# A two-pass mixture-of-experts block on one core: half tiles of two experts share a slot, in two column tiles of TensorE

## The chip, the cores and the metric

One core of a Trainium2 chip. The time of a run is the device time of the whole program in microseconds (us); all arithmetic on the path described here is float32.

## The reference, cut to what matters

The input is `x`, 4096 tokens (2 sequences of 2048) of 256 channels. Three layers follow one another, each on a layer-normed input and added to it:

```python
x = x + 0.5 * ffn(layernorm(x))     # mixture of 8 experts, one per token
x = x + recurrence(layernorm(x))    # 256 -> 64, three gated linear recurrences along the sequence, 64 -> 256
x = x + 0.5 * ffn(layernorm(x))     # the same mixture again

def ffn(x):                         # tokens xt [4096, 256]
    probs = softmax(xt @ Wr + br);  gate = max(probs);  idx = argmax(probs)
    h = relu((layernorm(xt) * ln_g + ln_b) @ W1[idx] + b1[idx])  # 256 -> 1024
    return (h @ W2[idx] + b2[idx]) * gate                        # 1024 -> 256
```

The inputs fix which expert each token gets. Worked out from the reference, tokens of each expert after each quarter of both sequences (the kernel's classes 0 to 3):

```text
first ffn     expert 0   1     2    3     4    5   6    7
  after c=0          95    8   366    7   503    0   0   45
  after c=1         173   12   768   10   993    1   0   91
  after c=2         252   13  1169   13  1483    2   0  140
  after c=3         332   17  1583   15  1969    2   0  178
second ffn
  after c=0          76   12   430    5   449    0   0   52
  after c=1         138   19   834    7   949    0   0  101
  after c=2         201   22  1229    9  1463    1   0  147
  after c=3         265   27  1637    9  1972    1   0  185
```

## The kernel before, in words

**Routing.** For every class of 1024 tokens (512 of each sequence) the kernel computes router logits on TensorE (`transposes`, `logits`, `turn_logits`), the argmax and the token's rank among its expert's tokens (`choose` L808, `ranks` L1583, `place` L846 on VectorE), and scatters the token rows into a region per expert in DRAM (`routed_rows`): `route` L641, four parts of two indirect DMAs each, issued by POOL. `counts` and `keep_counts` give the running counts per expert.

**Slots.** An FFN pass works in slots of 128 rows of one expert. `tables` (L871, six parts on VectorE) writes for each slot its expert, its first row and a mask for rows that are not there. Slots come in stages, so that a pass can begin before all classes are routed: `EARLY` gives the slots of the early stages, (9) in pass 0 and (4, 9, 8) in pass 1; the last stage takes what is left, partly filled tiles among it. Each stage's tables need the routing of one more class (in pass 0: classes 0 and 1, then all).

In slot `i`, SyncE loads the rows (`slot_rows` L460, ring of 5) and 1 MB of first weights (`slot_weights` L467, ring of 3 buffers, so the load of slot i waits for the first product of slot i-3); the second weights of all 8 experts stay in SBUF. VectorE normalises (`norm` L1171); TensorE transposes the 128x256 tile (`turn_input` L1686, L1692); ScalarE applies gain and offset (`affine`, L1431). TensorE's first product (L1705) holds a 128x128 block of weights and moves the 128 rows, so the hidden layer comes out with its channels on partitions; ScalarE and VectorE add the bias and clip, half each (`activate`, L1441 and L1185), and the second product (L1719) holds a block of the hidden layer and moves 256 columns of the second weights. VectorE adds the bias, the gate and the residual (`finish` L1189), and POOL scatters the rows to `x_middle` or the output (`store`, L655). TensorE's order in a slot is: transposes of slot i+1, first product of i, second product of i-1. Every float32 matmul is two records in the trace, a transpose is one.

**Order of the rest.** Everything else is "beside work": routing, tables and the recurrence (down projection `down` L1595, gates L1603, `project`, `norms`, `spread`, `up`, with `convolve`, `gate_input`, `scan` on VectorE). Lists of numbers at the top (L22 to L69) place each step by hand: a slot has a place (`PLACE`), a place is 2 steps on VectorE, ScalarE and POOL (before and behind the activation, on POOL behind the first half of the first product) and 8 on TensorE (behind each quarter of the two products), and each step is divided in `SUB` = 24. So 1704 on POOL is step 71, the second half of place 35. At a stage boundary TensorE holds back half of the last second product until the next stage's first rows are there (`begin_stage` L1737); SyncE waits for the stage's tables before its first weights (`next_weights` L476) and for its scatters before its first rows (`next_rows` L481), in order with all else in its queue. The recurrence begins at place 20 of pass 0 and ends in pass 1's early stages; its results of class c must be routed before pass 1's stage c begins. The banks 4 to 7 and the buffer `rec` belong to the beside work.

## Time and profile before

| | |
|---|---|
| runs before | 711.96, 714.51, 716.04 us, median 714.51 |
| profiled execution | 711.34 us, span of the trace 709.6 us |
| TensorE busy | 658.8 us, 93% of the span |
| VectorE, ScalarE, POOL busy | 409.5, 271.4, 172.2 us |
| mean granted TensorE clock | 0.966 |
| first products (L1705) | 2368 records, 286.9 us busy |
| second products (L1719) | 1184 records, 276.3 us busy |
| weights, 1 MB each | 82 loads by SyncE, median 5.2 us from issue to landing |

TensorE's busy time is that of its matmul records, which overlap; the chain of waits shows how far apart they really start. The span is from the first to the last instruction; the device time has 1.7 us more.

### The profile page before, as it was taken

What the parts mean: (1) busy time and instruction counts of PE and PEld (TensorE: products, weight loads), DVE (VectorE), ACT (ScalarE), POOL (GpSimd) and SP (SyncE); (2) the same over time, 40 slices, a digit from 0 to 9 for tenths busy, and PEclk for the clock granted to TensorE, in tenths of its full rate; (3) what the DMA queues carried; (4) which work ended last, traced back from release to release, by engine and by line L of the source; (5) the groups of instructions that cost most, each with busy time, mean ns of one, the idle gap of its engine ahead of it and who ended that gap; (6) DMA issues with size and microseconds to landing.
All of it is one profiled execution on the core that took longest, in us unless ns stands there. A gap on an engine that the chain in (4) does not pass through costs nothing.

```text
span 709.6 us, 15541 instructions
## 1 busy us (share of the span) xinstructions
PE 658.8 (93%) x4420; PEld 576.8 (81%) x4420; DVE 409.5 (58%) x1427; ACT 271.4 (38%) x642; POOL 172.2 (24%) x177
## 2 busy tenths in 40 slices
PE   7649999999999999999998979999799999999993
PEld 5548888999978878797777857889589989999992
DVE  7756672333355677777787757787567623333331
ACT  4214221332235656544654437554343223222220
POOL 4733443111111121033302330124212521111111
PEclk9559999999999999999999999999999999999998
DMA  8969785865563544437336164423553666452530
GB/s 287 303 200 394 275 269 184 264 204 164 189 222 129 169 150 142 142 88 242 101 99 232 70 237 144 150 82 120 178 202 133 196 200 203 152 202 96 178 125 14
DMA packets 59920, 126.51 MB, mean 178 GB/s; under 512 B 8106, under 2 KB 36661, under 8 KB 59701
## 3 DMA queue, kind: packets, MB, share of 16 engines
q1 hardware_dynamic: 53204, 108.50, 46.7%
q0 software_dynamic: 6624, 16.92, 6.5%
q8 instruction: 42, 0.69, 0.4%
q14 instruction: 50, 0.40, 0.2%
HBM read 106.36 MB, written 20.35 MB: 179 GB/s over the span
## 4 chain that ended last, share of the span: by engine, by line
PE 66%; DVE 12%; issue 7%; DVEq 5%; DMA 3%; POOL 2%; ACT 1%; SPq 0%; POOLq 0%; ACTq 0%
PE bank L1705 30%; PE bank L1719 28%; PE bank L1692 2%; POOL routed_rows L646 2%; DMA pay<-routed_rows 2%; DVE st L759 2%; DVEq L400 1%; DVE rec L1095 1%; PE bank L1642 1%; PE bank L1609 1%; DVE act_t L1185 1%; DVE rec L1071 1%; PE bank L1616 1%; DVE y_b L1194 1%; PE bank L1547 1%
## 5 line engine op out<-in xcount | busy, mean ns | idle before, releaser
L1705 PE MATMUL bank<-mn_t,w 128*128 128x128 f32 x2368 | 286.9, 277 | 3.9 <-ACT mn_t L1431 1.9
L1705 PEld LDWEIGHTS bank<-mn_t,w 128*128 128x128 f32 x2368 | 276.2, 193 | 15.3 <-issue 10.3
L1719 PE MATMUL bank<-w,act_t 128*128 x1184 | 276.3, 383 | 5.7 <-DVE y_b L1194 5.3
L1719 PEld LDWEIGHTS bank<-w,act_t 128*128 128x128 f32 x1184 | 218.2, 191 | 42.8 <-issue 17.0
L1431 ACT ACTIVATE mn_t<-bank,vec 128x128 f32<-128x128 f32 x152 | 61.5, 455 | 242.6 <-PE bank L1692 242.6
L1185 DVE TENSOR_SCALAR act_t<-bank,vec 128x128 f32<-128x128 f32 x296 | 83.3, 344 | 104.0 <-PE bank L1705 89.8
L1441 ACT ACTIVATE act_t<-bank,vec 128x128 f32<-128x128 f32 x296 | 84.9, 369 | 69.4 <-PE bank L1705 69.3
L1194 DVE TENSOR_TENSOR y_b<-bank,b_all 128x256 f32<-128x256 f32 x74 | 31.4, 425 | 105.4 <-PE bank L1719 94.7
L655 POOL DMA_INDIRECT x_middle<-res,pay x37 | 36.9, 997 | 216.9 <-DVE res L1201 182.2
L655 POOL DMA_INDIRECT out_x<-res,pay x37 | 36.9, 996 | 205.8 <-DVE res L1201 171.8
L646 POOL DMA_INDIRECT routed_rows<-rows,dest x64 | 64.6, 1010 | 56.3 <-PE bank L1705 27.1
L1176 DVE TENSOR_SCALAR mn<-pay 128x256 f32<-128x256 f32 x78 | 31.8, 408 | 20.7 <-DMA pay<-routed_rows 20.3
L1692 PE MATMUL bank<-ident,mn 128*128 128x128 f32 x152 | 30.3, 282 | 13.9 <-DVE mn L1176 9.2
L638 POOL TENSOR_TENSOR inv_std<-var_eps,minus_half 128x16 f32<-128x16 f32 (+1 forms) x12 | 31.0, 2581 | 48.6 <-DVE var_eps L769 35.0
L1201 DVE SCALAR_TENSOR_TENSOR res<-y_b,pay 128x256 f32<-128x256 f32 x74 | 35.8, 484 | 7.2
L1692 PEld LDWEIGHTS bank<-ident,mn 128*128 128x128 f32 x152 | 20.4, 145 | 22.7 <-issue 9.7
L759 DVE BATCH_NORM_STATS2 st<-rows 128x6 f32<-128x256 f32 x96 | 33.7, 414 | 2.6 <-DMA rows<-in_L_attn_h 0.7
L1071 DVE SCALAR_TENSOR_TENSOR rec<-seq,lay,rec 128x512 f32<-128x512 f32 x36 | 27.0, 749 | 2.0 <-issue 0.2
L1335 ACT ACTIVATE xn_t<-bank 128x512 f32<-128x512 f32 x32 | 17.9, 604 | 18.8 <-PE bank L1547 18.7
L1547 PE MATMUL bank<-ident,rows 128*128 128x128 f32 x128 | 20.4, 312 | 0.7 <-ACT xn_t L1335 0.6
L1547 PEld LDWEIGHTS bank<-ident,rows 128*128 128x128 f32 x128 | 17.2, 163 | 3.5 <-issue 2.4
L1373 ACT ACTIVATE rec<-bank,lay 64x512 f32<-64x512 f32 x24 | 16.4, 683 | 9.5 <-PE bank L1609 9.2
(212 smaller groups left out, 459.7 us busy)
## 6 DMA issues: line engine op xcount, KB each, us to landing
w<-in_L_ffn_W SPq DMA_DIRECT2D x82, 1024.0 KB, 5.2
pay<-routed_rows SPq DMA_DIRECT2D x78, 130.0 KB, 2.1
rows<-in_L_attn_h SPq DMA_DIRECT2D x8, 512.0 KB, 7.0
rows<-x_middle SPq DMA_DIRECT2D x8, 512.0 KB, 5.1
routed_rows<-fill SPq DMA_DIRECT2D x2, 1040.0 KB, 7.7
routed_rows<-rows,dest POOLq DMA_INDIRECT x64, 3.5
b_all<-in_L_ffn_b SPq DMA_DIRECT2D x1, 1024.0 KB, 12.0
x_middle<-res,pay POOLq DMA_INDIRECT x37, 2.6
```

The source lines that it names most:

```text
L646: g.indirect_dma_start(out=routed[f], out_offset=bass.IndirectOffsetOnAxis(ap=dest[:, t:t + 1], axis=0), in_=rows[:, t * RW:(t + 1) * RW], ...
L655: g.indirect_dma_start(out=x_out if p else x_mid, out_offset=bass.IndirectOffsetOnAxis(ap=pay[p][i % RING][:, C_ID:C_ID + 1].bitcast(I32), ...
L759: v.bn_stats(st[:, jj * 6:jj * 6 + 6], tile_of(c, b, j, 0, D))
L1185: last = v.tensor_scalar(act_t[i % 2][:, c * P:(c + 1) * P], b_hid[1][:, c % 4 * P:(c % 4 + 1) * P], vec[:, ds(eb + c, 1)], 0.0, ALU.add, ...
L1194: v.tensor_tensor(y_b[i % 2][:, :], b_out[i % 2], b2_all[:, ds(eb * (D // FC), D)], ALU.add).then_inc(m_yk[p], 1)
L1201: v.scalar_tensor_tensor(out=res[p][i % 2][:, :], in0=y_b[i % 2][:, :], scalar=a[:, C_GATE:C_GATE + 1], in1=a[:, 0:D], op0=ALU.mult, op1=A ...
L1431: last = a.activation(mn_t[p][i % 2][:, k * P:(k + 1) * P], b_in[i % 2][:, k * P:(k + 1) * P], ACT.Identity, scale=vec[:, V_G + k:V_G + k ...
L1441: last = a.activation(act_t[i % 2][:, c * P:(c + 1) * P], b_hid[0][:, c * P:(c + 1) * P], ACT.Relu, bias=vec[:, ds(eb + c, 1)])
L1547: last = t.transpose(bk[cc][n % 2][:, j * P:(j + 1) * P], tile_of(c, b, j, k * P, P), ident[:, :])
L1692: last = t.transpose(b_in[i % 2][:, k * P:(k + 1) * P], mn[p][i % 2][:, k * P:(k + 1) * P], ident[:, :])
L1705: last = t.matmul(b_hid[half][:, c % 4 * P:(c % 4 + 1) * P], w1[i % W1S][:, k * F + c * P:k * F + (c + 1) * P], mn_t[p][i % 2][:, k * P:(k ...
L1719: last = t.matmul(b_out[i % 2], act_t[i % 2][:, c * P:(c + 1) * P], w2[:, ds(eb * (WE // FC) + c * D, D)], start=c == 0, stop=c == FC - 1)
```

## The change

Per pass, three slots become pair slots (`PAIR_AT`: the second, fifth and eighth slot of the last stage). A pair slot takes 64 rows of each of two experts. A new function `pairs` in front of the last tables finds the experts whose remaining number of 64-row halves is odd, orders them ahead of the others, and gives the first six of the order one half each; the rest of the tables is made from what is left. The early stages are (7) and (5, 9, 8) instead of (9) and (4, 9, 8).

In a pair slot the first product turns round: the rows are stationary (64 columns for each expert) and the weights move, 512 columns at a time, each expert in its own column tile (output partitions 0 to 63 and 64 to 127). The hidden layer comes out with its rows on partitions, is copied raw to `rec` (`keep_hidden`), turned by 8 transposes into banks 4 and 5 (`turn_hidden`), and then gets bias and relu in 64-column pieces, since the two halves have different biases (`activate_pair`, in the next slot). The second product has 64 stationary columns per expert, again in two column tiles; the second expert's second weights are loaded once more into `rec` (1 MB), the first's are in place. A pair slot loads two first-weight buffers of the ring. All lists of places are written anew with `SUB` = 96.

```diff
-SUB = 24
+SUB = 96
...
-R_SCATTER = [[[None, None, None, None], [None, None, None, None], [72, 120, 168, 216], [264, 312, 360, 408]],
-    [[1560, 1608, 1656, 1704], [2040, 2088, 2136, 2160], [2472, 2520, 2568, 2616], [2856, 2904, 2952, 3000]]]
-TABLE_PARTS = [[[None, None, None, None, None, None], [169, 192, 240, 264, 288, None]], [[1584, 1609, 1633, 1682,
-    1683, 1728], [2066, 2088, 2112, 2113, 2116, 2281], [2497, 2544, 2568, 2569, 2593, 2616], [2881, 2904, 2905,
-    2952, 2953, None]]]
+R_SCATTER = [[[None, None, None, None], [None, None, None, None], [289, 480, 481, 672], [673, 864, 865, 1056]],
+    [[6240, 6432, 6433, 6624], [8544, 8545, 8640, 8641], [10272, 10464, 10465, 10560], [11232, 11424, 11425,
+    11616]]]
+TABLE_PARTS = [[[None, None, None, None, None, None], [577, 768, 864, 960, 1056, None]], [[6433, 6528, 6624, 6626,
+    6720, 6722], [8546, 8640, 8641, 8642, 8644, 8645], [10369, 10464, 10560, 10562, 10563, 10564], [11329, 11520,
+    11616, 11712, 11808, None]]]
...
-    EARLY = ((FULL,), (4, 9, 8))
+    HALF = P // 2
+    PAIRS = 3
+    HALVES = 2 * PAIRS
+    PAIRED = HALVES * HALF
+
+    EARLY = ((FULL - 2,), (5, 9, 8))
...
+    PAIR_AT = [[FIRST[p][-1] + 1 + 3 * k for k in range(PAIRS)] for p in range(FFNS)]
...
+        w2_b = rec[:, 0:WE]
+        raw_h = rec[:, WE:WE + F]
+        b_turn = [bank[4], bank[5]]
...
+            def pair_second_weights(p, i):
+
+                k = PAIR_AT[p].index(i)
+                eb = expert_of_half(sp, p, i, 1)
+                if k:
+                    sp.wait_ge(m_y[p], PAIR_AT[p][k - 1] + 1)
+                sp.dma_start(w2_b.rearrange("p (c d) -> p c d", c=FC),
+                             w2_rows[ds(eb * (F // FC), F), :].rearrange("(c p) d -> p c d", p=P)).then_inc(s_w, 16)
...
+            def pairs(f):
...
+                v.tensor_scalar(odd_i, odd_i, HALF.bit_length() - 1, 1, ALU.logical_shift_right, ALU.bitwise_and)
...
+                v.scalar_tensor_tensor(out=key, in0=odd, scalar=float(2 * E), in1=e_desc[:, :], op0=ALU.mult, op1=ALU.add)
...
+                    if last:
+                        pairs(f)
...
+            def keep_hidden(p, i):
+                dve.wait_ge(m_h[p], halves_before(p, i) + 2)
+                v.tensor_copy(raw_h[:, F // 2:F], b_hid[1][:, :]).then_inc(m_a[p], 1)
+
+            def activate_pair(p, i):
+                experts = [expert_of_half(dve, p, i, h) for h in range(2)]
+                dve.wait_ge(m_h[p], halves_before(p, i) + 4)
+                for c in range(FC // 2, FC):
+                    for h in range(2):
+                        lo = h * HALF
+                        last = v.tensor_scalar(act_t[i % 2][:, c * P + lo:c * P + lo + HALF],
+                                               b_turn[1][:, c % 4 * P + lo:c % 4 * P + lo + HALF],
+                                               vec[:, ds(experts[h] + c, 1)], 0.0, ALU.add, ALU.max)
+                last.then_inc(m_a[p], 1)
...
+                if is_pair(p, i):
+                    k = q % 2
+                    for h in range(2):
+                        on = slice(h * HALF, (h + 1) * HALF)
+                        lo = k * P + h * HALF
+                        last = t.matmul(b_hid[half][on, :], mn_t[p][i % 2][:, lo:lo + HALF],
+                                        w1[loads[h] % W1S][:, k * F + half * (F // 2):k * F + (half + 1) * (F // 2)],
+                                        start=k == 0, stop=k == KD - 1)
...
+            def turn_hidden(p, i):
+
+                for half in range(2):
+                    pe.wait_ge(m_a[p] if half else m_b[p], activations_before(p, i) + 1)
+                    for c in range(FC // 2):
+                        o = half * (F // 2) + c * P
+                        last = t.transpose(b_turn[half][:, c * P:(c + 1) * P], raw_h[:, o:o + P], ident[:, :])
+                    last.then_inc(m_h[p], 1)
...
+                    for c in range(q * 2, q * 2 + 2):
+                        t.matmul(b_out[i % 2][0:HALF, :], act_t[i % 2][:, c * P:c * P + HALF],
+                                 w2[:, ds(eb * (WE // FC) + c * D, D)], start=c == 0, stop=c == FC - 1)
+                        last = t.matmul(b_out[i % 2][HALF:P, :], act_t[i % 2][:, c * P + HALF:(c + 1) * P],
+                                        w2_b[:, c * D:(c + 1) * D], start=c == 0, stop=c == FC - 1)
```

`keep_hidden` and `activate_pair` have twins on ScalarE for the first half of the hidden layer. `turn_hidden` stands on TensorE behind the second product of the slot before. Divided by `SUB`, the scatters of class 1 in pass 1 stood in steps 85, 87, 89 and 90 and now stand in 89, 89, 90 and 90, with the boundary's step being 90 in both; those of class 2 stood in 103, 105, 107 and 109 and now in 107, 109, 109 and 110, the boundary's step being 110. The tables of the same classes ended their part 4 in steps 88 and 108, and now do so in 90 and 110. In pass 0 the scatters end in step 11 instead of 17, and the tables' part 0 stands in step 6, before slot 3's activation, instead of step 7, behind it.

## Rows read from the trace of the kernel before

**Rows 1.** Stretches: us, busy PE, PEld, DVE, ACT, POOL; PE clock; DMA
```profile
197.00:381.00 184.00, 178.82 (x1200) 147.92 (x1198) 132.34 (x412) 99.07 (x199) 38.50 (x32) 1.00 0.46 153
381.00:424.00 43.00, 38.95 (x254) 32.90 (x255) 28.79 (x107) 18.42 (x42) 13.19 (x13) 0.95 0.46 160
...
513.50:694.30 180.80, 179.70 (x1239) 166.03 (x1237) 78.36 (x275) 52.27 (x153) 33.55 (x32) 1.00 0.51 166
```

**Rows 2.** Chain of waits, a quiet stretch; start us, us, what
```profile
614.79 3.57 PE bank L1705 x32
618.36 3.46 PE bank L1719 x16
621.82 0.22 PE bank L1692 x2
622.04 3.57 PE bank L1705 x32
```

**Rows 3.** The page's groups of instructions
```profile
L1441 ACT ACTIVATE act_t<-bank,vec 128x128 f32<-128x128 f32 x296 | 84.9, 369 | 69.4 <-PE bank L1705 69.3
...
L655 POOL DMA_INDIRECT x_middle<-res,pay x37 | 36.9, 997 | 216.9 <-DVE res L1201 182.2
L655 POOL DMA_INDIRECT out_x<-res,pay x37 | 36.9, 996 | 205.8 <-DVE res L1201 171.8
...
L1335 ACT ACTIVATE xn_t<-bank 128x512 f32<-128x512 f32 x32 | 17.9, 604 | 18.8 <-PE bank L1547 18.7
```

**Rows 4.** Chain of waits around the first down projection
```profile
202.04 0.87 PE bank L1547 x8
202.91 1.79 PE bank L1705 x16
204.70 1.87 PE bank L1599 x8
...
207.56 1.09 PE bank L1705 x8
```

**Rows 5.** Instructions of the down projection (L1599)
```profile
L1599 PEld LDWEIGHTS bank<-xn_t,down_t x32: 133/136/137, 204.6 to 407.8; 128*64 128x64 f32 x32
L1599 PE MATMUL bank<-xn_t,down_t x32: 592/592/643, 204.6 to 408.3; 128*64 128x512 f32 x32
```

**Rows 6.** Chain of waits, an up projection in two row tiles
```profile
290.81 1.06 PE bank L1642 x8
```

**Rows 7.** Timeline of VectorE, 44 to 125 us
```profile
55.44 0.23 DVE L838 TENSOR_TENSOR hit<-hit,e_desc 128x64 f32<-128x64 f32 x1
55.73 0.22 DVE L840 TENSOR_REDUCE first<-hit 128x8 f32<-128x64 f32 x1
...
77.07 0.41 DVE L1176 TENSOR_SCALAR mn<-pay 128x256 f32<-128x256 f32 x1 [1.86 <-DMA pay<-routed_rows]
...
81.24 0.19 DVE L906 TENSOR_TENSOR seg_x<-cnt,done 128x32 f32<-128x32 f32 x1
...
102.65 0.24 DVE L969 TENSOR_SCALAR tab_off<-slot_v,part_no 128x30 int32<-128x30 f32 x1
```

**Rows 8.** Timeline of TensorE, 80 to 130 us
```profile
81.28 3.74 PE L1705 MATMUL bank<-mn_t,w 128*128 128x128 f32 x32
```

**Rows 9.** Timeline of SyncE's queue, 40 to 125 us
```profile
118.78 2.92 SPq L465 DMA_DIRECT2D pay<-routed_rows  x3
```

**Rows 10.** Timeline of POOL, 404 to 426 us
```profile
411.79 0.98 POOL L646 DMA_INDIRECT routed_rows<-rows,dest  x1 [0.31 <-issue]
```

**Rows 11.** Timeline of SyncE's queue, 404 to 426 us
```profile
413.52 1.52 SPq L472 DMA_DIRECT2D w<-in_L_ffn_W  x2
415.88 2.54 SPq L465 DMA_DIRECT2D pay<-routed_rows  x3
```

**Rows 12.** Timeline of VectorE, 404 to 426 us
```profile
422.68 0.41 DVE L1176 TENSOR_SCALAR mn<-pay 128x256 f32<-128x256 f32 x1 [4.21 <-DMA pay<-routed_rows]
```

**Rows 13.** Waits of TensorE; us in total, times, longest
```profile
PE bank L1692 <- issue: 4.7, 2, 2.4
```

More of the change, by code:

```diff
@@ L382, in column_of, with is_pair, pairs_before, entry @@
             return rows_bcj[:, :, c, :, col]
+        def is_pair(p, i):
+            return i in PAIR_AT[p]
+        def pairs_before(p, i):
+            return sum(at < i for at in PAIR_AT[p])
+        def entry(p, i):
+            return i - pairs_before(p, i)
+        def half_of(p, i, h):
+            return 2 * PAIR_AT[p].index(i) + h
+        def pair_weights_landed(p, i):
+            return (EAGER + p * PAIRS + PAIR_AT[p].index(i) + 1) * 16
+        def loads_of(p, i):
+            u = i + pairs_before(p, i)
+            return [u, u + 1] if is_pair(p, i) else [u]
+        def slot_of(p, u):
+            return next(i for i in range(SLOTS[p]) if u in loads_of(p, i))
+        def rows_landed(p, i):
+            both = sum(at % RING == i % RING for at in PAIR_AT[p] if at <= i)
+            return (i // RING + 1 + both) * 16
+        def halves_before(p, i):
+            return 2 * (i + pairs_before(p, i))
+        def activations_before(p, i):
+            return i + pairs_before(p, i)
+        def activated(p, i):
+            return activations_before(p, i) + 1 + is_pair(p, i)
         def tables_at(p, s):
@@ L537, in between_passes @@
                 used = slots_used(sp, 0)
-                for i in range(EARLY[1][0]):
+                for i in range(RING - 1):
                     next_rows(1, i)
@@ L880, in tables @@
                 i0 = FIRST[f][s]
+                slots = i0 + PAIRS if last else i0
                 rw, tb, of = (t[f][:, i0:i0 + n] for t in (tab_row, tab_b, tab_off))
@@ L936, in tables @@
                     if last:
[L937 removed]
+                        v.tensor_scalar(tab_used[f][:, :], seg_end[:, m - 1:m], float(slots), None, ALU.add)
                     dve.drain()
```

300 lines of the change are left out of this document (217 added, 83 removed).

## The prediction

> **What bounds the kernel now.** I read the busy time by stage first. Outside the start and the tail TensorE has nearly no idle time: 178.82 of 184 us where the recurrence runs beside the slots, 179.70 of 180.8 us in the last stage; 38.95 of 43 us around one stage boundary is the weakest stretch, and what follows the last slot at 694.3 is a tail that the change leaves alone [rows 1]. So time comes out of this kernel by taking TensorE work out, and goes back in wherever TensorE is made to wait. The chain of waits then gives the price of a slot in a quiet stretch: two transposes 0.22 us, first product 3.57, second product 3.46, one slot every 7.25 us (614.79 to 622.04) [rows 2]. Each pass runs 37 slots, as the 37 stores into each output say [rows 3].
>
> **How many slots go.** This is arithmetic on the table of counts (reference section). I followed the table code: full 128-row tiles first, experts in order. In pass 0 the seven early slots take one tile of expert 0 and six of expert 2. Left are 204, 17, 815, 15, 1969, 2, 0, 178 rows, which is 4, 1, 13, 1, 31, 1, 0, 3 half tiles: six odd. The six experts with an odd number give one half each to the three pair slots; 24 whole slots are left, so 7 + 3 + 24 = 34. In pass 1 the 22 early slots take 1, 9, 11 and 1 tiles of experts 0, 2, 4 and 7. Left are 137, 27, 485, 9, 564, 1, 0, 57 rows, that is 3, 1, 8, 1, 9, 1, 0, 1 halves: again six odd, 9 whole slots left, 22 + 3 + 9 = 34. The same counting gives 37 and 37 for the kernel before, as the trace has it [rows 3]. **Removed:** 12 whole slots (6 per pass) x 7.25 = 87.0 us of TensorE.
>
> **Price of a pair slot.** Six are added. First product: 8 matmuls of 64 stationary columns and 512 moving, alternating between the two column tiles. The kernel before has that very shape in the down projection: 4 such matmuls are 8 records of 592 ns each, spaced so that all 8 take 1.87 us [rows 4, 5]. The neighbours give the streaming time: 16 records that move 128 columns take 1.79 us, 0.112 each, so 512 columns take about 0.43, and 8 one behind another would take 3.4 us. So two run side by side: four rounds of 0.43 and 0.16 for changing over; the step back to whole-array matmuls adds 0.20 (1.09 us for 8 records against 0.89, half of 1.79) [rows 4]. The pair's first product is 8 rounds, 3.41 us + 0.36. Second product: 16 matmuls of 64 stationary and 256 moving columns. No row has this shape. Bound below: side by side throughout, 16 rounds of 0.213 = 3.41 us + 0.36. Bound above: one behind another, 6.8 + 0.36. I take the lower, because its nearest row (same 128 rows by 64 columns, only longer) runs side by side, and 256-wide matmuls in two row tiles do 8 records in 1.06 us where one behind another needs 1.73 [rows 4, 6]. Turning the hidden layer: 8 transposes, 0.87 us as in the recurrence's group of 8 [rows 4]. With the input's 0.22 a pair slot is 3.77 + 3.77 + 0.87 + 0.22 = 8.63 us; six are 51.8 us. **TensorE in all: -87.0 + 51.8 = -35.2 us.**
>
> A rule of the Trainium skill speaks against the lower bound. In "TensorE: Matmul & The Clock Gate", section "The mechanism" of Part 3, LDWEIGHTS overlaps matmuls in flight only where the row group differs; column tiles share all rows. The down projection's loads (137 ns) disagree, since 1.87 us leaves no room for eight of them [rows 4, 5]; what it would cost if it held for 256 columns is a rival below.
>
> **What lies beside.** The two copies of the raw hidden layer (128x512, ScalarE and VectorE; ScalarE's 128x512 copies take 604 ns [rows 3]) run under the 3.46 us of the previous slot's second product. The 8 narrow activations per engine cost at most 8 x 0.369 = 3.0 us [rows 3] under the next slot's first product of 3.57. If that cover failed, a pair would cost 1 or 2 us more, up to 10 us for six. Queue and traffic: a pair brings one more 1 MB load (the second expert's second-product weights) and needs two first-product loads; the second of these can go out when the first product of two slots before is done, some 11 us before use, where the page gives 5.2 us as the median from issue to landing. I take nothing for it. SP's and POOL's other work is moved, not added, and that is where the cost is.
>
> **The work placed anew.** Four places.
> (a) Pass 0, slot 3. The routing of the last quarter and part 0 of the tables with the new pairing function now stand before slot 3's activation, not after it. The pairing is about 25 small operations in 17 dependent steps; two such steps are 0.29 us apart (55.44 to 55.73), so 5 us, and part 0 is 2 us (81.24 on) [rows 7]. VectorE is free of the norm at 77.6 [rows 7]; the activation ends near 86.3 where it used to end before 81.24. TensorE starts the next first product at 81.28 [rows 8] and wants that bank half way through, at 83.1: **+3 us**.
> (b) Pass 0's boundary comes after 7 slots instead of 9. Before, the tables were complete at 102.9 [rows 7], and the rows went out only at 118.78, when the last scatter had landed [rows 9]. Now SP stands in the wait for the tables from slot 4's iteration on, and three weight loads and the rows queue behind it; scatters are packed two parts to a half slot. Tables end near 101, rows near 104 to 108, boundary near 107: **+1 us**.
> (c) Pass 1's boundary after the first quarter. Four scatter parts (8 DMAs of 0.98 + 0.31 us [rows 10]: 10.3 us on POOL) now stand in the last slot and the boundary itself, where two stood; and the tables' parts 1 to 4 move from one slot ahead into the boundary. From the last scatter (411.79) to the normalised rows (422.68) it took 10.9 us, with weights issued at 413.52 ahead of the rows at 415.88 [rows 10 to 12], and TensorE stood at this boundary and the next for 4.7 us in two pieces, the longer of 2.4 [rows 13]. The later scatters alone add 5 us, the later tables put two weight loads behind them too; some 4 us more TensorE work stands there to cover. **+6 us** (0 to 10).
> (d) Pass 1's next boundary, in front of slot 14 (slot 13 before), is packed in the same way, with one part more than before in the last half slot and the tables at the boundary, beside a projection chain that now also runs there; the other 2.3 us stood here [rows 13]. **+2 us** (0 to 6).
> Nothing else: the gap between the passes has the same chain through it as before. Idle in all: +12 us; lower bound -3 (denser work could also fill the waits that exist), upper +24.
>
> **Sum.** The profiled execution took 711.3 us (span 709.6 and 1.7 around it), 3.2 under the median of 714.5. -35.2 + 12 = -23.2: 688 against its own time, 691 against the median. I give 691.
>
> **The rivals.** (1) *The idle time does not grow*: the new placement covers its own cost, and all of -35.2 arrives, 679. For it: pair slots stand where no recurrence runs, and the last stretch is full [rows 1]. Against it: (a) is a plain queue on VectorE. (2) *Weight loads exposed*: in a round of two 0.213 us matmuls two loads of 0.137 stand in series, 0.27 against 0.213; 16 rounds x 0.06 x 6 = 6 us, 697. If no load overlapped at all, 16 x 0.27 x 6 = 26 us, 717: no change. That is what the skill's sentence on row groups would make of it; rows 4 and 5 speak against it. (3) *The boundaries take the gain*: each of the three remade boundaries waits 8 us longer for tables and rows and then runs its first matmuls at a lower clock (granted 0.95 around 381 to 424 [rows 1]): about 707. (4) *Slower: the column tiles do not run side by side.* Place: both products of the pair slots. Price 2 x 3.41 us per pair, 41 us, 732. It decides from 4 us per pair on (24 over six), that is when two tiles together gain less than 1.26 times. Only a difference between 512 and 256 columns, or moving data from two weight buffers, could do it. (5) *The change does not pair what it says*: each odd expert fewer is one slot of 7.25 us; with four odd ones in each pass it would be 29 us, 720. The counts say six; only near-ties in the routing could alter a count.
>
> **How the numbers follow.** Forecast 0.50 (own range 685 to 698), rival 1 0.26, rival 2's small form 0.08, its large form 0.03, rival 3 0.07, rival 4 0.04, rival 5 0.02. The range 678 to 702 takes in the forecast, rival 1 and the small form of 2, and leaves out about 0.18. About 0.5% (3.6 us) is what a measurement can tell from no change. Faster: 0.92; same: rival 2's large form and half of 5, 0.03; slower: rival 4 and the rest, 0.05.
>
> **What would show it.** 34 stores per pass instead of 37. In a pair slot: 16 first-product records in about 3.6 us, 32 second-product records in about 3.6, 8 transposes in 0.9. TensorE busy time lower by 35 us. VectorE's hidden-layer activation of slot 3 ending 5 us late with TensorE waiting for it; waits of 6 to 12 us before the input transposes of pass 1's slots 5 and 14. Wrong would be: pair slots of 12 us and more, 35 or more slots, or new waits outside the four places.

## The result, and the profile after

The change makes the kernel **slower**: median 746.11 us (739.62 to 747.41) against 713.83 us before on the same chip, ratio 1.0433 [1.0364, 1.0501]. On a second chip, beside four of the experiments, it took 734.9 against 710.73, ratio 1.0330 [1.0294, 1.0365]. The forecast was 691 us with a range of 678 to 702. The profiled span is 745.5 us against 709.6, 35.9 longer, at a mean granted clock of 0.928 against 0.966.

The page of the changed kernel: TensorE's line (busy us, share of the span, instructions), three lines of the 40 slices, and the groups that answer to [rows 3]. L1931 is the first product (L1705 before), L1965 the second (L1719), L750 the store (L655).

```profile
PE 644.3 (86%) x4168; PEld 536.3 (72%) x4168; DVE 412.3 (55%) x1465; ACT 263.3 (35%) x634; POOL 167.5 (22%) x171
...
PE   7459798899999999999769957999759899998893
...
PEclk9659999999999999999879997999958999998997
...
L1931 PE MATMUL bank<-mn_t,w 128*128 128x128 f32 x1984 | 249.3, 283 | 20.7 <-DVE act_t L1363 7.9
...
L1965 PE MATMUL bank<-w,act_t 128*128 x992 | 240.3, 392 | 16.4 <-DVE y_b L1381 16.1
...
L750 POOL DMA_INDIRECT out_x<-res,pay x34 | 34.6, 1017 | 242.9 <-DVE res L1388 152.9
L750 POOL DMA_INDIRECT x_middle<-res,pay x34 | 35.3, 1038 | 215.9 <-DVE res L1388 178.6
```

The 34 stores per pass are there: the slots were saved as counted. TensorE was busy 658.8 us and is busy 644.3, so 14.5 less where 35 was forecast, and its time out of work went from 51 to 101 us. In place of a nearly solid row of nines the slices show dips to 5 to 7 between 47 and 75% of the span. Idle time in front of the two products was 3.9 and 5.7 us before, and is 20.7 and 16.4.

The pair slot itself, in the timeline of TensorE of the changed kernel (start us, us, engine, line, operation, what it writes and reads, count):

```profile
123.11 0.38 PE L1903 MATMUL bank<-ident,mn 128*128 128x128 f32 x2
123.51 3.65 PE L1922 MATMUL bank<-w,mn_t 128*64 128x512 f32 x16
127.10 3.72 PE L1965 MATMUL bank<-w,act_t 128*128 x16
130.66 1.04 PE L1943 MATMUL bank<-ident,rec 128*128 128x128 f32 x8
...
135.41 0.43 PE L1957 MATMUL bank<-w,act_t 128*64 x1
135.42 0.43 PE L1959 MATMUL bank<-rec,act_t 128*64 128x256 f32 x1
135.68 0.38 PE L1957 MATMUL bank<-w,act_t 128*64 x1
...
139.02 0.44 PE L1903 MATMUL bank<-ident,mn 128*128 128x128 f32 x2
```

The first product takes 3.59 us (123.51 to 127.10), the second 3.61 (135.41 to 139.02, 32 records, two at a time), the turn 0.87 (130.66 to 131.53). With 0.22 for the input these pieces are 8.29 us. The steps between whole-array and column-tiled matmuls come on top: from the pair's input (123.11) to the input behind its second product (139.02) pass 15.91 us, in which the two products and the input of plain slots stand too. Less 7.25 for those, a pair slot costs 8.66 us, against 8.63 in the forecast. What the change is about works as forecast. The loss is elsewhere.

The same kernel by stage (columns as in [rows 1]):

```profile
50.30:117.30 67.00, 58.37 (x378) 52.71 (x378) 45.09 (x191) 15.86 (x48) 28.37 (x24) 0.94 0.81 277
...
376.20:453.00 76.80, 59.32 (x362) 45.97 (x359) 51.92 (x171) 34.56 (x66) 17.88 (x14) 0.88 0.33 116
453.00:559.00 106.00, 92.93 (x593) 77.74 (x593) 69.22 (x214) 50.37 (x101) 21.04 (x18) 0.90 0.35 121
559.00:629.30 70.30, 65.05 (x420) 59.79 (x421) 38.30 (x162) 17.09 (x50) 18.37 (x17) 0.94 0.52 170
629.30:735.30 106.00, 97.94 (x635) 78.88 (x633) 35.02 (x117) 27.33 (x89) 11.90 (x13) 0.95 0.52 179
```

Set against the kernel before, stage by stage, with 7.25 us for each slot more or fewer (a pair slot is counted as one slot, so that three of them alone would show as about +4):

| stretch | before | after | over |
|---|---|---|---|
| pass 0, early slots | 74.2 us, 9 slots | 67.0, 7 slots | +7.3 |
| pass 0, further slots | 241.0, 27 slots | 228.2, 26 slots | -5.6 |
| last slot of pass 0 to pass 1's first input | 17.4 (362.4 to 379.8) | 30.7 (345.5 to 376.2) | +13.3 |
| pass 1 to its first boundary | 43.4, 4 slots | 76.8, 5 slots | +26.2 |
| to the second boundary | 90.1, 9 slots | 106.0, 9 slots | +15.9 |
| to the third | 66.0, 8 slots | 70.3, 8 slots | +4.3 |
| last stage, to the last slot's input | 107.6, 15 slots | 93.7, 11 slots | +15.1 |

The third boundary was not among the prediction's four places. The pairing function of pass 1 stands in the stage before it: TensorE waits 2.06 us for an activation at 598.21. The whole of the changed kernel also starts 3.2 us later (first slot's input at 48.69 instead of 45.52); on the second chip it does not (45.10).

At the first boundary of pass 1 the timeline of TensorE shows this (in brackets the idle time before, and what ended it):

```profile
433.60 1.80 PE L1965 MATMUL bank<-w,act_t 128*128 x4 [3.74 <-DVE y_b L1381]
...
441.38 1.06 PE L1773 MATMUL bank<-xn_t,wr_c 128*32 128x512 f32 x8 [2.16 <-ACT xn_t L1524]
...
447.20 1.75 PE L1827 MATMUL bank<-rec,rec_t 128*128 128x512 f32 x2 [2.29 <-DVE rec L1250]
453.05 0.66 PE L1903 MATMUL bank<-ident,mn 128*128 128x128 f32 x2 [4.11 <-issue]
```

and SyncE's queue this, the three weights behind the tables and the rows behind them:

```profile
393.11 51.71 SPq L557 DMA_DIRECT2D w<-in_L_ffn_W  x3
445.66 2.56 SPq L545 DMA_DIRECT2D pay<-routed_rows  x3
```

At the second boundary TensorE has nothing but the recurrence's own chain, each link waiting for another engine:

```profile
544.02 3.78 PE L1965 MATMUL bank<-w,act_t 128*128 x8 [7.53 <-DVE y_b L1381]
547.59 1.91 PE L1827 MATMUL bank<-rec,rec_t 128*128 128x512 f32 x2
550.76 1.05 PE L1832 MATMUL bank<-half_sel,rec 128*128 128x2 f32 x8 [1.26 <-ACT rec L1577]
...
555.16 2.08 PE L1853 MATMUL bank<-up_t,rec 64*128 64x256 f32 x8 [1.85 <-DVE rows L1281]
559.07 0.66 PE L1903 MATMUL bank<-ident,mn 128*128 128x128 f32 x2 [1.83 <-issue]
```

Eight second-product records take 3.57 us there (544.02 to 547.59); in a quiet stretch sixteen take 3.46 [rows 2]. The granted clock of those 3.6 us is 0.50. So such a wait is paid twice, once as a wait and once in matmuls at half the cadence behind it (granted clock 0.88 and 0.90 in these two stages, 0.96 and 0.98 before). Not every wait is: behind the 2.16 us at 441.38 the clock is 1.00. The slower records are most of the reason why busy time fell by only 14.5 us: at the mean record of the kernel before, the two products of the whole slots would be busy 17.7 us less than they are.

### The profile page after: what moved, and what is told of

Its sections match the earlier page's. It is cut to its first block, busy times and chain, and to the rows that moved or that the text cites. A ratio compares the mean times of both kernels' runs of the same rounds, so it can differ in the third digit from the quotient of the medians.

```text
span 745.5 us, 14980 instructions
## 1 busy us (share of the span) xinstructions
PE 644.3 (86%) x4168; PEld 536.3 (72%) x4168; DVE 412.3 (55%) x1465; ACT 263.3 (35%) x634; POOL 167.5 (22%) x171
## 4 chain that ended last, share of the span: by engine, by line
PE 56%; DVE 14%; issue 11%; DMA 6%; DVEq 5%; ACT 2%; POOL 2%; another core or an unknown queue 1%; SPq 1%; ACTq 0%; POOLq 0%
PE bank L1931 21%; PE bank L1965 20%; PE bank L1957 3%; PE bank L1922 2%; DVE st L854 2%; PE bank L1903 2%; POOL routed_rows L741 1%; DVEq L456 1%; DMA x_middle<-res,pay 1%; DMA rows<-x_middle 1%; PE bank L1827 1%; DVE y_b L1381 1%; DVE act_t L1363 1%; PE bank L1820 1%
## 5 line engine op out<-in xcount | busy, mean ns | idle before, releaser
L1931 PE MATMUL bank<-mn_t,w 128*128 128x128 f32 x1984 | 249.3, 283 | 20.7 <-DVE act_t L1363 7.9
L1931 PEld LDWEIGHTS bank<-mn_t,w 128*128 128x128 f32 x1984 | 238.9, 198 | 28.5 <-issue 13.1
L1965 PE MATMUL bank<-w,act_t 128*128 x992 | 240.3, 392 | 16.4 <-DVE y_b L1381 16.1
L1965 PEld LDWEIGHTS bank<-w,act_t 128*128 128x128 f32 x992 | 187.4, 196 | 56.2 <-issue 33.2
L1620 ACT ACTIVATE mn_t<-bank,vec 128x128 f32<-128x128 f32 x140 | 56.7, 458 | 220.9 <-PE bank L1903 192.5
L1363 DVE TENSOR_SCALAR act_t<-bank,vec 128x128 f32<-128x128 f32 x248 | 69.8, 345 | 73.3 <-PE bank L1931 54.6
L1648 ACT ACTIVATE act_t<-bank,vec 128x128 f32<-128x128 f32 x248 | 70.7, 368 | 63.1 <-PE bank L1931 58.7
L750 POOL DMA_INDIRECT out_x<-res,pay x34 | 34.6, 1017 | 242.9 <-DVE res L1388 152.9
L750 POOL DMA_INDIRECT x_middle<-res,pay x34 | 35.3, 1038 | 215.9 <-DVE res L1388 178.6
L1381 DVE TENSOR_TENSOR y_b<-bank,b_all 128x256 f32<-128x256 f32 x62 | 26.3, 424 | 94.1 <-PE bank L1965 84.0
L1331 DVE TENSOR_SCALAR mn<-pay 128x256 f32<-128x256 f32 x72 | 29.4, 410 | 21.0 <-DMA pay<-routed_rows 17.7
L1903 PEld LDWEIGHTS bank<-ident,mn 128*128 128x128 f32 x140 | 18.8, 148 | 18.5 <-issue 15.1
L1957 PE MATMUL bank<-w,act_t 128*64 x96 | 24.6, 414 | 5.3 <-DMA rec<-in_L_ffn_W 3.9
L1524 ACT ACTIVATE xn_t<-bank 128x512 f32<-128x512 f32 x32 | 17.8, 594 | 23.4 <-PE bank L1758 21.0
L1758 PE MATMUL bank<-ident,rows 128*128 128x128 f32 x128 | 21.8, 323 | 3.9 <-DMA rows<-x_middle 2.0
L1959 PE MATMUL bank<-rec,act_t 128*64 128x256 f32 x96 | 24.6, 414 | 0.0
```

The costliest lines, as they stand in the source:

```text
L750: g.indirect_dma_start(out=x_out if p else x_mid, out_offset=bass.IndirectOffsetOnAxis(ap=pay[p][i % RING][:, C_ID:C_ID + 1].bitcast(I32), ...
L1363: last = v.tensor_scalar(act_t[i % 2][:, c * P:(c + 1) * P], b_hid[1][:, c % 4 * P:(c % 4 + 1) * P], vec[:, ds(eb + c, 1)], 0.0, ALU.add, ...
L1381: v.tensor_tensor(y_b[i % 2][:, :], b_out[i % 2], b2_all[:, ds(eb * (D // FC), D)], ALU.add).then_inc(m_yk[p], 1)
L1620: last = a.activation(mn_t[p][i % 2][:, k * P:(k + 1) * P], b_in[i % 2][:, k * P:(k + 1) * P], ACT.Identity, scale=vec[:, V_G + k:V_G + k ...
L1648: last = a.activation(act_t[i % 2][:, c * P:(c + 1) * P], b_hid[0][:, c * P:(c + 1) * P], ACT.Relu, bias=vec[:, ds(eb + c, 1)])
L1903: last = t.transpose(b_in[i % 2][:, k * P:(k + 1) * P], mn[p][i % 2][:, k * P:(k + 1) * P], ident[:, :])
```

## The experiments

I had three suspects: the order of SyncE's queue, which the forecast had put at nothing; the new places; and a third that I had not thought of, that pass 0 can't be shortened because the recurrence and not the slots sets its end. The runs fall into four groups, each on one chip with its own time of before: 710.8 us for the first three, 710.73 for the next three and the changed kernel again, and 711.36 or 712.9 for the rest. Between groups the ratio to the kernel before is the safer measure.

**Pair slots at the old places.** The slots, tables and `pairs` of the change, with the stages and all lists of the kernel before.

```diff
-    EARLY = ((FULL - 2,), (5, 9, 8))
+    EARLY = ((FULL,), (4, 9, 8))
...
-SUB = 96
+SUB = 24
```

> Pair slots as changed, but the early stages (9) and (4, 9, 8), the lists of places with SUB = 24 and the slots beside which the middle rows are loaded are those of the kernel before (one unused slot is appended to pass 0 so that the places of pass 1 fall where they did). Theory P (the placement cost the time: of some 70 us lost against slots that are 35 us cheaper, about 47 lie where the recurrence stands beside the slots, at the two boundaries whose tables and scatters were moved into the boundary): this kernel is faster than before, 685 to 700 us. Rival F (the chain of the recurrence needs its slots: with 34 slots instead of 37 in pass 0 there is too little beside it, whatever the placement): 720 to 745. In both, TensorE's chain has three pair slots per pass of 8.6 us each.

Measured: 720.0 us, before 710.8, ratio 1.0123 [1.0076, 1.0169]. Without the new places the change is still no gain, but 15 us of the changed kernel's excess (734.9 less 720.0, on two chips whose times of before agree within 0.1 us) come with them. Theory P failed, and the time lies at the edge of rival F's. Some 40 us are missing in the slots' own account: +9.2 us where six pair slots for 12 whole ones should give -35.2 less a few.

**Pass 1's pairs as plain slots.** The changed kernel, its three pair slots of pass 1 run as whole slots with the first expert's weights: no column tiles, no second loads, the same number of slots. The second expert's rows of those slots are computed with the first expert's weights.

```diff
-    PAIR_AT = [[FIRST[p][-1] + 1 + 3 * k for k in range(PAIRS)] for p in range(FFNS)]
+    TABLE_AT = [[FIRST[p][-1] + 1 + 3 * k for k in range(PAIRS)] for p in range(FFNS)]
+    PAIR_AT = [TABLE_AT[0], []]
```

> The changed kernel, but in pass 1 the three pair slots run as ordinary slots: rows of two experts are loaded, all 128 are computed with the first expert's weights, and neither the second loads nor the transposes of the hidden layer are made; half of their rows thus get the wrong expert, in the last layer alone. Arithmetic of a pair slot as forecast (8.63 against 7.25 us): 3 x 1.4 = 4 us less. Theory Q (the last stage lost a further 10 us because second weights and weight loads stand behind the wait for stored rows on SyncE's queue): another 10, in all 14 less than the changed kernel, about 732. If pair slots themselves were dear on TensorE (rival), the same total would come, but with long transposes or products in the trace of the changed kernel.

Measured: 717.8 us, ratio 1.0093 [1.0061, 1.0124], 17 us below the changed kernel by ratio. Three pair slots cost 3 x 1.4 = 4.2 us more than plain ones (8.66 less 7.25). The last stage takes 93.7 us (629.3 to 723.0) in the first profile of the changed kernel, 91.5 in the one on the second chip, and 78.5 (615.1 to 693.6) here. So 9 to 11 us of it are not the price of the slots, and the loads are what is left to suspect.

**Loads first.** In the changed kernel SyncE's queue shows where it hurts:

```profile
659.00 0.38 SPq L557 DMA_DIRECT2D w<-in_L_ffn_W  x1
665.93 1.74 SPq L537 DMA_DIRECT2D pay<-routed_rows  x2
668.67 0.15 SPq L526 DMA_DIRECT2D rec<-in_L_ffn_W  x1
```

The pair's second weights (L526) stand behind the rows (L537), which wait for a buffer of the ring of rows. They leave at 668.67, and TensorE, ready for them at 670.5, waits 3.95 us, until 674.46. Then its 32 records take 6.16 us (to 680.62) instead of 3.6; the granted clock is 0.50 up to 679.2. The edit asks for weights ahead of rows:

```diff
+                    if is_pair(1, i + 1):
+                        pair_second_weights(1, i + 1)
                     rows_behind_weights(1, i)
                     rows_in_turn(1, i + RING - 1)
-                    if is_pair(1, i + 1):
-                        pair_second_weights(1, i + 1)
```

The same stands in pass 0, and the tail asks for a slot's own weights before the rows of two slots on.

> The changed kernel with two moves on SyncE's queue: a pair's second weights are asked for before the rows of the slot four ahead, and the first weights of slot 31 of pass 1 before the rows of slot 33. Theory Q: the waits of 3.95 us on rec and of 2.93 us before slot 31's first product go, with the half-clock stretches behind them (2.6 and 1.6 us): 9 to 11 us less than the changed kernel, 735 to 737. Rival (the loads are late because the DMA rings are full): no change beyond 2 us.

Measured: 722.5 us, ratio 1.0141 [1.0093, 1.0189], 12.4 us below the changed kernel's 734.9 and a little more than the 9 to 11 us of theory Q. The forecast of 735 to 737 had started from the first chip's 746. The last stage takes 83.6 us (615.7 to 699.3), 10.1 less than in the first profile and 7.9 less than in the second. The wait for `rec` is gone.

**Both, old places and loads first.**

> Pair slots in both passes on the old places (as e1), and on SyncE's queue the pair's second weights ahead of the rows of the slot four on. Theory Q (the waits on rec of 8.1 us in three pieces in e1 come from that order): 6 to 10 us less than e1, 710 to 714. If the loads are late for lack of DMA bandwidth: 718 to 720, as e1.

Measured: 710.38 us, before 710.73, ratio 1.0001 [0.9976, 1.0027]. This is what theory Q said. Ratios of the four kernels with pair slots in both passes:

| | rows first | loads first |
|---|---|---|
| new places | 1.0330 | 1.0141 |
| old places | 1.0123 | 1.0001 |

Load order is worth 9.6 us here, 12.4 there (8.7 and 13.4 by ratio); the new places cost 12.1 us with loads first (722.5 against 710.4; 10 by ratio). The intervals leave some 4 us open on each. What is left, six pair slots and 12 whole slots fewer, gives nothing at all, where -35.2 had been forecast.

**Pairs in one pass only**, on that kernel (`ON` switches each pass's pair slots; the other pass has 37 whole slots as before).

```diff
-    LAST = [(T - t + E * (HALF - 1)) // P for t in TAKEN]
-    LAST[0] += 1
+    ON = (0, 1)
+    LAST = [30, 19]
```

> Old places, pair slots in pass 1 alone (37 slots in pass 0, 34 in pass 1), loads in the better order. Theory F2 (in pass 0 the slots only cover the chain of the recurrence, which ends pass 0 whatever the slots cost; behind the last boundary of pass 1 nothing stands beside the slots, so there 3 x 7.25 x 2 - 3 x 8.63 = 17.6 us fewer are fewer): 692 to 697 us, faster than the kernel before. Rival (pair slots give nothing anywhere, for want of loads or because of their own waits): 706 to 715.

> Old places, pair slots in pass 0 alone. Theory F2: the three slots saved come back as waits at the end of pass 0, where TensorE has the recurrence's chain and nothing beside it, and the pairing function costs 5 to 8 us in slot 3: 712 to 722 us, no faster than before. Rival (TensorE's work is what counts everywhere): 694 to 700.

Measured: pairs in pass 1 alone 699.5 us, ratio 0.9846 [0.9814, 0.9877]; pairs in pass 0 alone 722.0, ratio 1.0161 [1.0125, 1.0197]. -11.2 and +11.2 add to the zero of both, so the two passes can be looked at one by one. Both rivals fell. Pass 0 came out as theory F2 said, at its upper edge; pass 1 gave 2.5 us less than its range. The timeline of TensorE with pairs in pass 0 alone, from the last slot's second product (352.08) to pass 1's first input (389.19):

```profile
352.08 3.72 PE L1968 MATMUL bank<-w,act_t 128*128 x16
...
364.30 2.07 PE L1830 MATMUL bank<-rec,rec_t 128*128 128x512 f32 x2 [2.81 <-DVE rec L1253]
367.64 1.87 PE L1835 MATMUL bank<-half_sel,rec 128*128 128x2 f32 x8 [1.26 <-ACT rec L1580]
...
380.65 1.86 PE L1789 MATMUL bank<-pick,lg_t 128*128 128x16 f32 x8 [4.24 <-DVE rows L1284]
...
389.19 0.66 PE L1906 MATMUL bank<-ident,mn 128*128 128x128 f32 x2
```

and the same chain in the kernel before, with halves of the last slots' products between its links:

```profile
374.62 1.02 PE L1616 MATMUL bank<-rec,rec_t 128*128 128x512 f32 x2
...
377.29 0.95 PE L1621 MATMUL bank<-half_sel,rec 128*128 128x2 f32 x8
379.75 0.41 PE L1692 MATMUL bank<-ident,mn 128*128 128x128 f32 x2 [1.51 <-DVE mn L1176]
```

**This is the main finding.** Before, slots 34 to 36 of pass 0 were the cover of the recurrence's last steps. From the input in front of slot 33's first product to pass 1's first input the kernel before takes 51.6 us (328.2 to 379.8) with three more slots in it; with pairs in pass 0 it takes 48.3 (340.9 to 389.2) without them. Three slots of 7.25 us, 21.8 us, bring back 3.3. The chain runs bare, its eight records in 1.87 us instead of 0.95 (granted clock 0.50 there, 0.77 over the whole gap). Meanwhile the rest of pass 0 is longer: the same input stood at 328.2 and stands at 340.9. Of these 12.7 us 5.8 lie in front of pass 0's boundary, where TensorE waits 4.93 us behind `pairs`, and 6.9 behind it, where three pair slots at 1.4 us each are 4.2. So pass 1 begins 9.4 us later. Whether the chain could be begun earlier in pass 0, so that it ends with fewer slots, was not tried.

**The pairing function off the critical path.** With pairs in pass 1 alone, TensorE waited 3.34 us at 560.27 for an activation behind `pairs`. The prediction had a term for the pairing function in pass 0, and none for this one. The edit spreads the last tables over free half slots (here and below, only the list that changes is shown):

```diff
-    [2881, 2904, 2905, 2952, 2953, None]
+    [2904, 2928, 2952, 2953, 2976, None]
```

> e5 (old places, pair slots in pass 1 alone, loads in the better order) with the last tables of pass 1 spread: the pairing function and part 0 stand behind slot 18's activation instead of before it, parts 1 to 4 in the following steps. In e5 TensorE waits 3.3 us for that activation and then runs 16 records in 3.6 us instead of 1.9. Theory (VectorE's queue in front of an activation, and the half clock behind the wait): both go, 5 us less than e5, 693 to 696 us. Rival (the pairing only moves the wait to another slot): within 2 us of e5.

Measured: **696.8 us**, before 711.36, ratio 0.9787 [0.9749, 0.9826]. It beats both kernels. Its TensorE is busy 92% of the span (639.7 of 696.6 us), at a granted clock of 0.968. How much of this the spreading brought is less sure: the two ratios' intervals overlap, and the profiled executions differ by only 0.6 us. In them the stage before the third boundary is 2.7 us shorter (68.6 against 71.3) and the last stage 2.2 us longer, where TensorE now waits 1.78 us for weights.

**The same in pass 0** (on the kernel with pairs in pass 0 alone; tables' part 0 from step 7 to 11, `pairs` in step 9).

> e6 (old places, pair slots in pass 0 alone) with the pairing function behind slot 4's activation and the parts of pass 0's tables in later steps, so that no activation waits for them. In e6 TensorE waits 4.9 us there and then takes 5.6 us for 16 records instead of 3.5. 7 us less than e6, 714 to 716. Theory F2 says that it goes no further: still not below the kernel before, although TensorE has 17.6 us less to do in pass 0, because the gap behind pass 0's last slot stays near 48 us (17.4 before). Rival (the pairing function in pass 0 was all that hid the gain): 700 or less.

Measured: 727.7 us, before 712.9, ratio 1.0218 [1.0164, 1.0271], against 1.0161 without it. A miss: no gain of 7 us. A loss isn't shown either. The intervals overlap, and the profiled executions differ by 3.9 us, all of which lies before pass 0's first input (49.32 against 45.40, on another chip). From there to the boundary it takes 82.0 us with the edit and 81.8 without. The wait behind `pairs` halved, from 4.93 to 2.47 us, but TensorE then waited for rows at the boundary. SyncE's queue, and the boundary on TensorE:

```profile
102.08 19.94 SPq L557 DMA_DIRECT2D w<-in_L_ffn_W  x3
128.62 0.35 SPq L545 DMA_DIRECT2D pay<-routed_rows  x1
```

```profile
131.34 0.66 PE L1906 MATMUL bank<-ident,mn 128*128 128x128 f32 x2 [5.76 <-issue]
```

Without the edit SyncE's three weight loads end 8.77 us after 105.52, the row load is issued at 124.50, and the boundary is at 127.18. With it the weights, behind the later tables, end at 122.02. POOL issues the last scatter at the same time in both (121.1), and the rows wait for it to land. Between 122 and 126 us the DMA engines are 92% busy here and 18% there, so the late weights may have held the scatter up; this was not tried. The gap between the passes is as wide as ever: 346.2 to 394.8, 48.6 us.

**What in the new places costs.** Three stages with the new places (first fence) and the old ones (second), both with loads first; the first row of each is the gap between the passes:

```profile
341.70:370.90 29.20, 20.86 (x119) 15.48 (x117) 19.01 (x80) 8.85 (x17) 9.76 (x10) 0.88 0.55 184
370.90:446.50 75.60, 59.39 (x363) 46.08 (x360) 51.93 (x171) 34.56 (x66) 17.89 (x15) 0.88 0.31 111
446.50:547.70 101.20, 91.96 (x594) 76.98 (x594) 69.25 (x213) 50.37 (x101) 20.99 (x18) 0.92 0.38 134
```

```profile
339.70:388.00 48.30, 33.83 (x173) 22.93 (x171) 34.02 (x107) 21.35 (x33) 11.50 (x9) 0.77 0.42 143
388.00:431.40 43.40, 38.91 (x255) 32.17 (x255) 29.40 (x109) 19.38 (x43) 13.59 (x12) 0.95 0.34 119
431.40:520.30 88.90, 82.51 (x560) 69.76 (x560) 65.11 (x210) 46.46 (x94) 20.37 (x18) 1.00 0.42 144
```

The new places take 19.1 us out of the gap by leaving part of the chain to pass 1. There it comes back: +32.2 us before the first boundary (7.25 of it is the slot more) and +12.3 before the second. (The two profiled executions lie 17.8 us apart, the medians 12.1, so the traces show somewhat too much.) Two edits asked which part of a boundary it is. The first makes the tables' parts 1 to 4 of classes 1 and 2 one step earlier, so that SyncE is not held by them:

```diff
-    [8546, 8640, 8641, 8642, 8644, 8645]
+    [8546, 8547, 8548, 8549, 8550, 8645]
```

> e3 (the changed kernel with the better order of loads) with the tables of pass 1's second and third stage pulled out of the boundary: their parts 1 to 4 stand in the step before it, behind the last activation. Theory T (the rows are late at these boundaries because SyncE issues two weight loads and the rows only once the tables are there): 6 to 10 us less than e3 at the two boundaries. Rival V (VectorE's queue is full there, and what is done earlier makes the result of the slot before later, on which TensorE also waits: 3.7 and 7.5 us on y_b in the changed kernel): within 2 us of e3.

Measured: 722.4 us, before 711.36, ratio 1.0160 [1.0120, 1.0200]: no change from 1.0141, as rival V said. The second boundary's rows went out at 532.99, early enough, but the tables' operations now stood ahead of the second product's bias on VectorE (TensorE waited 6.11 us for `y_b`), and the chain of `project`, `norms` and `up` ran on until 544.5. The second edit moves that chain behind the boundary. It is that of the recurrence's third layer for the last quarter of the tokens (entry 3 of each list, counted from 0; the expectation below calls it class 2):

```diff
-PROJECT = [..., [22944, 31968, 38784, 42432]]
+PROJECT = [..., [22944, 31968, 38784, 43008]]
```

The lists of the steps that follow it (squares, norms, `up` and its additions) move with it.

> e9 (the changed kernel, loads in the better order, tables ahead of the boundaries) with the end of the recurrence's third layer of class 2 (projection, squares, norms, up projection and its two additions) moved out of the boundary in front of slot 14 to behind it. In e9 the rows of slot 14 were asked for at 532.99, and TensorE stood in that chain until 544.5. Theory S (what holds a boundary is whichever of two serial chains ends last, the recurrence's or that of tables, loads and rows; moving one alone shows nothing): 5 to 8 us less than e9, 714 to 717. Rival (the chain's time comes back behind the boundary): within 2 us of e9, 722.

Measured: 737.3 us, before 712.9, ratio 1.0343 [1.0296, 1.0390], 15 us worse (13 by ratio; in the traces 2.7 of 13.0 lie before the first slot's input); a clear miss of both theories. The boundary came no earlier, and the stage behind it took 52.8 us (546.9 to 599.7) to the input that the other kernel reached in 43.2 (544.5 to 587.7). TensorE at the boundary:

```profile
537.32 3.78 PE L1968 MATMUL bank<-w,act_t 128*128 x8 [10.50 <-DVE y_b L1384]
546.93 0.66 PE L1906 MATMUL bank<-ident,mn 128*128 128x128 f32 x2 [5.83 <-issue]
```

The wait for `y_b` grew from 6.11 to 10.50 us, and the rows, asked for at 538.92, were normalised only at 546.42. VectorE had stood 5.55 us in front of its activation at 528.63, released by something that the profile does not name, so the tables and the weights behind them were late. The chain's records now stand among the new stage's slots, with waits of their own (1.07 and 2.21 us). What VectorE waited for stays open, and with it which of the two, if either, holds this boundary.

**TensorE kept in motion.** Eight matmuls of the identity with itself, whose result nobody reads, at each boundary of pass 1, on the 696.8 us kernel, to see whether the half cadence behind a wait can be bought off.

```diff
+                            if p == 1:
+                                in_motion(8)
                             pe.wait_ge(s_tab, tables_at(p, FIRST[p].index(i)))
```

> e8 with 8 matmuls of the identity (16 records, about 1.8 us) issued at each stage boundary of pass 1 in front of the wait for the next rows. In e5 the waits there are 2.2 to 2.3 us, and at the first boundary the 8 records behind it take 3.2 us instead of 1.9. Theory C (the half clock behind a wait is set off by the idle time, and is worth as much again): 1 to 3 us less than e8. Rival: the matmuls come on top where the wait is short: 0 to 3 us more.

Measured: 699.7 us, ratio 0.9838 [0.9799, 0.9876], against 0.9787 without. No gain, and rather a loss of 3 us (all four times lie above the four without), as the rival said. The first boundary with them; without them; and without them in the kernel that differs only in the later tables (pairs in pass 1 alone, 699.5 us):

```profile
424.67 0.41 PE L1906 MATMUL bank<-ident,mn 128*128 128x128 f32 x2 [1.12 <-issue]
424.92 1.89 PE L1968 MATMUL bank<-w,act_t 128*128 x8
```

```profile
423.12 0.52 PE L1906 MATMUL bank<-ident,mn 128*128 128x128 f32 x2 [1.19 <-issue]
423.44 3.51 PE L1968 MATMUL bank<-w,act_t 128*128 x8
```

```profile
424.89 0.41 PE L1906 MATMUL bank<-ident,mn 128*128 128x128 f32 x2 [2.22 <-issue]
425.13 1.89 PE L1968 MATMUL bank<-w,act_t 128*128 x8
```

Against the second fence the eight records take 1.89 us instead of 3.51, but the boundary comes 1.55 us later; at the next records (426.65 and 426.78) nothing is left of it. The third fence shows that even the 1.89 can't be put down to the added matmuls: behind a wait of 2.22 us, without them, the records take 1.89 as well. (The 3.2 us that the expectation gives for this kernel are those of the kernel before, at 423.65.) The second boundary came at 513.4 in both. The third came at 584.0 instead of 582.0: there is no wait for rows there, and the 16 records simply take their 1.8 us.

**The changed kernel again**, beside the experiments.

> The changed kernel itself, on this chip beside the others: 740 to 747 us. If it comes out near 733, a part of e3's gain of 24 us against the figure of 746 was the chip and not the order of the loads.

Measured: 734.9 us, ratio 1.0330 [1.0294, 1.0365], below the range, so a part of the step from 746 to 722.5 was indeed the chip. The excess has the same parts: the gap between the passes 346.0 to 375.9 and 75.4 us to the first boundary. By the experiments it is made of -11.2 (pairs in pass 1) + 11.2 (pairs in pass 0) + 12.1 (new places) + 12.4 (load order) = 24.5, and 24.2 was measured. Only the first two terms are tested by this: the last two are steps from one measured kernel to the next and must add up. On the first chip the excess was 32.3; the weights took 7.4 us (median) to land there and 5.5 here. That this is the cause of the 8 us between the chips was not tried. Nor were the new places tried without pair slots, since they count on three slots fewer in pass 0.

## Why the prediction was wrong

**Right:** the 12 slots removed, and 34 stores per pass; the price of a pair slot (8.66 us measured, 8.63 forecast); the activations and copies, hidden but for one wait of 1.3 us. Rival 4 (no column tiles side by side) and rival 5 fell. So did rival 2: even its small form, 16 rounds at 0.27, needs 4.3 us, and the 32 records took 3.61. The Trainium skill's sentence on row groups ("TensorE: Matmul & The Clock Gate", Part 3, "The mechanism") does not hold for these column tiles, which share all their rows.

**"TensorE in all: -35.2 us", taken as time.** This is the step that failed most. It holds only where a slot is what sets the end. In pass 1's last stage it is: three pair slots there brought 11.2 us, and 14.5 with `pairs` spread, of the 17.6 that is half of 35.2. In pass 0 it isn't. The sentence "Nothing else: the gap between the passes has the same chain through it as before" saw the chain, but not that its length was hidden by the very slots that were taken out. The row 178.82 of 184 us busy [rows 1] was read as proof that TensorE set the pace; it said only that slots and chain filled one another's gaps. Pass 0's half came to +11.2 instead of -17.6. Of these 28.8 us 18.5 are the uncovered chain (21.8 us of slots removed, 3.3 brought back); 5.8 stand in the early stage with `pairs` in it, for which (a) and (b) had +4; the rest is spread over the slots behind.

**"I take nothing for it", the pair's loads.** In SyncE's old order they cost 9.6 to 12.4 us, a small move in the tail included. The landing time had been compared with the time from a free buffer to its use (11 us against 5.2). The load does not leave when the buffer is free, but when SyncE has passed the row load in front of it, which waits for a ring.

**(a) +3 us.** The mechanism was right. TensorE waited 4.41 us for the activation at 91.82, then needed 2.90 us for 16 records instead of 1.79 and 4.09 for the 16 behind them instead of 3.46: about 6. With (b), where +1 was forecast, the early stage came out 7.3 us over, against 4. The same function in pass 1 had no term; its stage came out 4.3 us over, and with pairs in pass 1 alone 5.3 (71.3 against 66.0).

**(c) +6 and (d) +2 us.** Right in place, wrong in size: +26.2 and +15.9 in the first measurement. A part of it is the recurrence's chain, which the new places take out of the gap (19.1 us) and put here. The forecast added scatters and tables as queue time on POOL and SyncE (the queue rows above show that part: rows out at 445.66), and left out that tables and chain also stand ahead of `y_b` on VectorE (3.74 and 7.53 us), that the links of the recurrence's chain then run one after another with no slot beside them, and that long waits are followed by matmuls at half cadence. How the two stages' excess divides among these stays open: the two edits that each moved one of them gained nothing. Rival 3 named this mechanism, at 8 us for each boundary; with 0.07 it got too little, and its time of 707 too small a price.

The range was built from the bounds of single terms. The costs that weren't terms, the uncovered chain (18.5 us) and the loads (10 to 12), lie outside all of them.

## What to carry to other kernels

Before taking work off an engine that is 97% busy, ask what runs beside that work and how long this takes alone: if a serial chain through other engines ends with the last slot, a slot removed comes back as a wait. Here three slots of 7.25 us brought back 3.3. Take work out first where nothing else runs (here the three slots in pass 1's last stage gave 1.5%, and 2.1% with `pairs` spread), and ask of each new load where it stands in its queue, not only when its buffer is free. A busy-time saving is time saved only in stretches where the engine's next wait is for itself.

## What the runs showed of the hardware

- Two column tiles with 64 stationary columns each run side by side at both widths: 16 records of 512 columns in 3.59 us, 32 records of 256 columns in 3.61 us. The 32 weight loads of the second take 137 ns each, 4.4 us one behind another, so they run beside the matmuls.
- A wait of 4 to 8 us on the path was paid again behind it. After 4.41 us 16 records took 2.90 us instead of 1.79; after 3.95 us, in the changed kernel's last stage, 32 records took 6.16 instead of 3.61; after 7.53 us eight took 3.57 instead of 1.73. The granted clock was 0.63 over the first of these stretches, 0.50 in the first 4.7 us of the second and 0.50 in the third; 0.50 is the level of 1.2 GHz instead of 2.4. With pairs in pass 0 alone the gap between the passes ran at 0.77, and its groups of eight records took 1.87 us instead of 0.95.
- Waits of 1 to 3 us went both ways at the same place. At pass 1's first boundary eight records took 3.51 us behind 1.19 us of wait, 3.19 behind 2.37, and 1.89 behind 2.22. With 16 added records in front they took 1.89 too, so these runs don't show that adding matmuls keeps the clock up, and it gained no time.
